# One transformer block on one core: other order of the score, value and wide steps inside a group of four

## The reference

```
x = x + cross_attention(layernorm(x), context)    # 16 heads of 16; softmax over 4096 context tokens
x = x + linear_attention(layernorm(x))            # features exp(clip(proj)), causal, 16 heads
x = x + ffn(layernorm(x))                         # silu(x Wg) * (x Wu), then Wd; hidden 768
```

## Time and profile before

| | |
|---|---|
| median of three runs | 904.28 us (903.49 to 911.03) |
| the profiled execution | 905.16 us, of which the span from first to last instruction 903.4 us |
| PE busy | 842.8 us (93%) |
| ACT busy | 533.5 us (59%) |
| DVE busy | 425.4 us (47%) |
| POOL busy | 48.4 us (5%) |
| mean granted TensorE clock | 0.985 |

### The profile page before, as it was taken

The page is one execution under the profiler, slowest core; times in us unless marked ns, Lnnn a source line. Parts: engine busy times, 40 slices in busy tenths (PEclk is TensorE's granted clock), DMA queues, the critical chain, the costliest instruction groups (busy, mean ns, idle before and its releaser), DMA issues.

```text
span 903.4 us, 20695 instructions
## 1 busy us (share of the span) xinstructions
PE 842.8 (93%) x8881; PEld 581.3 (64%) x8881; DVE 425.4 (47%) x751; ACT 533.5 (59%) x579; POOL 48.4 (5%) x76
## 2 busy tenths in 40 slices
PE   6899999999899999999899999999989999888876
PEld 6666666666566666676566666676656667657655
DVE  7433245545544446534644446434744444203663
ACT  2378787776467675656566665757556666760111
POOL 1034000000000000000000000000000000000000
PEclk9799999999999999999999999999999999999999
DMA  7487664656133334336333442446333331201000
GB/s 242 150 260 236 229 199 153 210 190 187 57 141 141 118 141 163 130 109 184 130 118 141 141 141 94 142 140 178 127 140 141 109 142 56 71 25 24 1 1 15
DMA packets 58736, 120.08 MB, mean 133 GB/s; under 512 B 21520, under 2 KB 29712, under 8 KB 55120
## 3 DMA queue, kind: packets, MB, share of 16 engines
q1 hardware_dynamic: 56848, 114.31, 37.2%
q0 software_dynamic: 1792, 4.40, 1.9%
HBM read 78.84 MB, written 37.75 MB: 129 GB/s over the span
## 4 chain that ended last, share of the span: by engine, by line
PE 77%; DVE 9%; issue 5%; DMA 4%; ACT 3%; DVEq 1%; POOL 1%; SPq 0%; POOLq 0%; ACTq 0%
PE ps_o L777 24%; PE ps_s L789 16%; PE ps_pa L576 10%; PE ps_pa L621 10%; ACT probs L1066 2%; PE ps_pa L747 2%; DMA oscr<-y 2%; PE ps_pa L722 2%; PE ps_pa L713 1%; DMA y<-oscr 1%; PE ps_pa L699 1%; PE ps_pa L651 1%; PE ps_pa L734 1%; PE ps_pa L643 1%; DVE kparts L1105 1%
## 5 line engine op out<-in xcount | busy, mean ns | idle before, releaser
L1066 ACT ACTIVATE probs<-ps_s 128x1024 f32<-128x1024 f32 x512 | 496.7, 1023 | 262.8 <-PE ps_s L789 254.4
L777 PE MATMUL ps_o<-probs,values 128*17 128x256 f32 x4096 | 257.6, 386 | 0.3 <-ACT probs L1066 0.3
L789 PEld LDWEIGHTS ps_s<-qstack,kstack 64*128 64x128 f32 x2048 | 139.1, 185 | 102.4 <-ACT probs L1066 53.2
L789 PE MATMUL ps_s<-qstack,kstack 64*128 64x256 f32 x2048 | 193.5, 307 | 7.0 <-ACT probs L1066 7.0
L777 PEld LDWEIGHTS ps_o<-probs,values 128*17 128x17 f32 x4096 | 104.4, 98 | 100.3 <-issue 12.8
L1103 DVE TENSOR_SCALAR kparts<-ps_pa,b_heads 128x512 fp32r<-128x512 f32 x64 | 48.0, 750 | 122.1 <-PE ps_pa L576 122.1
L1120 DVE TENSOR_TENSOR values<-ps_pa,bv_pair 128x512 f32<-128x512 f32 x64 | 44.1, 690 | 84.7 <-PE ps_pa L621 84.3
L621 PE MATMUL ps_pa<-wv_hi,ctx_hi 128*128 128x256 f32 x256 | 79.5, 310 | 2.6 <-DVE wv_lo L1091 2.2
L621 PE MATMUL ps_pa<-wv_lo,ctx_hi 128*128 128x256 f32 x256 | 73.2, 286 | 0.0
L621 PE MATMUL ps_pa<-wv_hi,ctx_lo 128*128 128x256 f32 x256 | 73.1, 286 | 0.0
L576 PE MATMUL ps_pa<-ctx_hi,wk_hi 128*128 128x512 f32 x128 | 56.5, 441 | 0.0
(11 more groups left out here) (252 smaller groups left out, 792.2 us busy)
## 6 DMA issues: line engine op xcount, KB each, us to landing
kstack<-kscr SPq DMA_DIRECT2D x96, 512.0 KB, 5.3
kscr<-kparts SPq DMA_DIRECT2D x64, 512.0 KB, 2.7
ctx_raw<-ctxT SPq DMA_DIRECT2D x32, 512.0 KB, 6.6
qstack<-qscr SPq DMA_DIRECT2D x12, 256.0 KB, 3.4
qscr<-qparts SPq DMA_DIRECT2D x4, 512.0 KB, 4.4
xh<-x SPq DMA_DIRECT2D x4, 256.0 KB, 5.6
kstack<-kstack SPq DMA_DIRECT2D x2, 512.0 KB, 6.0
qstack<-ksample SPq DMA_DIRECT2D x4, 256.0 KB, 3.6
```

The lines of the kernel that those rows point to most:

```text
L777: last = mm(ps_o[32 * j:32 * j + DH + 1, g * S:(g + 1) * S], values[par][:, i, head_of_step(g, j), :], prob[:, j * S:(j + 1) * S], start=b ...
L789: last = mm(ps_s[s % 2][:, j * S:(j + 1) * S], kstack[par][rows, u, i * P:(i + 1) * P], queries[rows, u, :], start=True, stop=True)
L1066: nc.scalar.activation(probs[n % AHEAD][:, :], ps_s[n % 2][:, :], ACT.Exp, scale=float(DH) ** -0.5).then_inc(fast["exp_done"], 1)
```

## The change

A quad with a wide stage gets another order on PE: two score steps, the unit and the narrow stages of all four slots, the value steps up to this quad (four of them), one score step, the wide stage, one score step. Inside such a quad the unit now stands ahead of the wide stage in all cases. So that DVE meets them in the same order, three wide stages move within their quad, to its last slot: feat0 from step 32 to 35, feat2 from 48 to 51 (behind pv0), A4 from 64 to 67. ACT's part of each feat stage comes after the last exponential of its quad. The order of TAIL, by which the last batch's stages run, changes in one place: pv0 comes ahead of feat2.

```diff
 AT = { ...
-      "feat0": 32, "feat1": 38, "A0": 42, "A1": 46, "feat2": 48, "pv0": 50, "A2": 54, "A3": 58, "pv1": 60, "feat3": 62,
-      "A4": 64, "A5": 70, ...
+      "feat0": 35, "feat1": 38, "A0": 42, "A1": 46, "pv0": 50, "feat2": 51, "A2": 54, "A3": 58, "pv1": 60, "feat3": 62,
+      "A4": 67, "A5": 70, ...
-ACT_BEHIND = {n: 1 - AT[n] % 2 if AT[n] // QUAD in WIDE_QUADS else QUAD - 1 - AT[n] % QUAD for n in FEATS + GATES}
+ACT_BEHIND = {n: QUAD - 1 - AT[n] % QUAD for n in FEATS + GATES}
...
-            def fast_slot(b, p, s):
+            def fast_slot(b, p, s, wide=True):
...
                 for name, clock in stages_at(b, p * STEPS + s):
-                    products(fast, [name], clock)
+                    if wide or name not in WIDE:
+                        products(fast, [name], clock)
...
                         if b and (p * STEPS + s) // QUAD in WIDE_QUADS:
-                            for half in (0, 2):
-                                for t in (0, 1):
-                                    fast_scores(b, q, s + half + t)
-                                for t in (0, 1):
-                                    fast_slot(b, p, s + half + t)
-                                values_up_to(n + half)
+                            for t in (0, 1):
+                                fast_scores(b, q, s + t)
+                            for t in range(QUAD):
+                                fast_slot(b, p, s + t, False)
+                            values_up_to(n)
+                            fast_scores(b, q, s + 2)
+                            for t in range(QUAD):
+                                for name, clock in stages_at(b, p * STEPS + s + t):
+                                    if name in WIDE:
+                                        products(fast, [name], clock)
+                            fast_scores(b, q, s + 3)
```

## The result

The changed kernel takes 939.73 us (median of four runs, 937.51 to 941.83), the kernel before beside it 906.18 (903.49 to 911.03). The ratio is 1.036, 95% interval 1.031 to 1.042: slower. I had forecast slower and 929, with a range of 918 to 937. The direction and the main cost were right, the size was not: 33.6 us between the medians against my 24.7, and the time is 2.7 us beyond the range. The profiled execution took 940.29 us, its span is 938.6; against the profiled execution before (905.16, span 903.4) that is 35.1.

A forecast was written before the change was run, and what follows sets the result against it. PE's own sequence was taken as the bound (93% busy). Per batch 12.6 - 1.5 - 1.8 - 1.5 = +7.8 us, three batches +23.4, tail +1.3: +24.7, giving 929 us, range 918 to 937.

The forecast's parts named there:

- Step 6: ACT and DVE in the new order: waits covered, unit behind wide stage with 0.8 us to spare; no cost counted.
- step 2: Wide stages in key-unit quads no longer wait for DVE to take keys from PSUM: gain 1.8 us per batch.
- Rival (b): Units behind wide stages wait for DVE, up to 1 us in a third of quads: 942 us; 6 in 100.
- Rival (c): Clock falls from PE idling, half of the 36 quads at the lower level: 69 us on top, 999; 3 in 100.
- Step 5: Score step n+5 behind each wide stage waits for exponential n+3: 1.05 us each, 12.6 us lost per batch.
- the 0.10 us: Part of the cost behind each wide stage: a score step after a wait costs 0.43, not 0.33, weights not loaded ahead.
- Step 1: Quads 8 to 20: 13 groups of value steps instead of 25, 0.13 us each: gain 1.5 us per batch.
- Step 3: Waits at score step 211 in quad 20 (0.64) and for exponential 192 in quad 16 (0.9) go: 1.5 us per batch.
- Step 4: PE's 1.11 us wait before feat0 for quad 7's keys stays, at quad 8's value unit: no change counted.
- Step 7: Last batch's tail: pv0 ahead of feat2 delays DVE's clip and A2's output: cost 1.3 us once.

The follow-up runs named there:

- the half exponential: Changed kernel, exponential of step n+3 in each of the 36 wide quads takes only half its tile: 920.53 us, before 905.24, ratio 1.019.
- the paired order: Changed kernel with score step n+3 ahead of the wide stage, which is now last in its quad: 929.80 us, before 905.24, ratio 1.029.
- D: Theory that in quads 8, 12, 16 DVE's first value output waits for the quad's own last value step; changed kernel without this wait: 928.84 us.
- the experiment on the value output: Changed kernel, DVE's output of a chunk's first value unit waits for eight value steps of the earlier chunk, not sixteen: 928.84 us, ratio 1.028.

## Why the prediction was wrong in size

**Where the 35 us are.** Between the two profiled executions: three stretches of 9.4 us, 28.3. Two lower-clock stretches in them, 3.0. The same once more in quads 26 and 27 of batch 3, 1.4. From the first score step of the last quad to the end of the span, 100.5 us (838.09 to 938.6) against 97.35 (806.09 to 903.4), 3.1, of which 1.4 are the order and 1.7 I put down to the clock. The rest, -0.7, is elsewhere. My sum had 23.4 for the stretches and 1.3 for the tail.

**Step 6 failed.** It said "The moved stages feat0, feat2 and A4 bring no instruction and no DMA more", which is true, and step 2 took the PE work between unit and wide stage (1.85 + 0.24 us) as enough to cover DVE's output of the unit in every quad. So the sum had nothing for a wait there. In quads 8, 12 and 16 it is not enough. `fast_values_out` waits for all value steps of the chunk before (`pv_done`), since it overwrites their buffer, and in the new order the last of these stand in the same quad, behind the unit. The old order had two or four value steps ahead of the unit. So the wide stage came 0.6 us late in quads 8 and 12 and 0.7 in quad 16, in each of three batches: 6.0 us by the experiment. With them the sum would have been 30.7 of the 33.6 us between the medians. I had looked for the waits of PE in the new order, and for one of ACT's, but not for those of DVE. Rival (b) had the right engine at the wrong place (units behind wide stages, its own 0.8 us to spare held).

**Rival (c) came, in a small form.** I gave the clock 3 in 100, all or nothing: 69 us. What happens is between: single short stretches at the lower level, some 1.5 us each, in two of three batches and in the tail. In numbers, the changed kernel ran at 0.973 to 0.978 in all nine runs, the kernel before at 0.975 to 0.988. I had leaned on one tail row with a clock of 1.00 and PE idle for 6 of 20 us; that row was true of one execution, and other executions of the kernel before go down to 0.975. With the value output's wait mended it is 0.977 to 0.985, with value steps behind the wide stage 0.981 to 0.983. Some 6 us between the two profiled executions hang on this; the sum had no term for it. That the waits of the changed kernel are the cause is not shown: with the old tail and the same waits three runs of four had 0.980 to 0.983, and the kernel with three waits mended, whose stretches leave PE idle for 1.1 us only, ran at 0.975 to 0.987. The Trainium skill ("TensorE: Matmul & The Clock Gate", A second HAM failure mode: psum-queue depth-cycling) says that short, frequent idling between groups of matmuls can make the clock swing. The two executions agree in direction: 0.50 was granted inside a stretch that had stayed at 1.00 in all three batches before. The price in this kernel is a few us.

**Step 5 was right for this order, and not the whole rule.** 1.62 us and 0.43 were measured as forecast, the half exponential gives its 0.43 us back twelve times per batch, and the waits vanish with two value steps between n+3 and n+5. But the paired order shows a second bound, which step 5 rightly set aside for its own order ("The exponential n+2 does not add"): n+2 to n+5 must hold two exponentials, 2.54 us, so that work between n+3 and n+5 alone need not end the wait. And the 0.10 us do not belong to the wait, as the last section shows; a lone score step costs them more than the second of a pair, wait or not. With D taken out, the stretch is 7.4 us longer than before, against my 7.8. That is close in part by luck: I had 0.24 us for the score step ahead of an A stage and 0.74 for the stage, and they cost 0.34 and 0.57.

**Steps 1, 3, 4 and 7 held, and step 2 but for what it took as covered.** Four value steps cost 1.85; an A stage in a key quad starts 0.34 behind its score step; quad 20's wait between 210 and 211 and quad 16's for exponential 192 are gone from the timeline; the value unit of quad 8 waits for the keys 1.0 us; the tail's order costs 1.4.

**What stays open.** Why the clock falls at one place and not at another was not tried: a filler matmul in the waits would need a free PSUM tile, and in these quads all of this kernel's are in use. Nor is it shown that idling lowered the clock here; the runs with the old tail speak against it. The 2.9 us between the medians that neither my sum nor the value output explains I put down to the clock, without a proof.

## What to carry to other kernels

With two tiles in turn between two engines, write down two distances for each new order: from a producer's step to the one that overwrites its tile, to compare with one step of the consumer plus the latencies (1.62 us here), and from the step before it, to compare with two (2.54); a quad of four steps needs other work in both of its gaps, not in one. When a step is moved, go through the waits of each engine that has a part in it, and ask of each semaphore what now stands in front of its last increment; a buffer's "all that used it are done" is the easiest to miss, and here it asked for more than is overwritten. And a kernel that sits at 97% busy still has waits worth naming: three of 0.6 to 1.1 us, mended together, gave 0.7%, a third less in the stretches than their sum, as the next wait took its share.

## What the runs showed of the hardware

A score step whose wait ends with an exponential costs 0.43 us to the next group instead of 0.33. It does so in each of the 36 quads. But it is no price of the wait: a score step that stands alone and waits for nothing costs as much in front of another kind of group, 249.79 - 249.35 = 0.44 in the experiment on the value output. 0.33 is the second of two score steps in a row (0.67 for both). The Trainium skill ("TensorE: Matmul & The Clock Gate", Step-by-step: what each phase is for) says that TensorE pulls weight loads ahead of matmuls in flight; the trace agrees, in that the weights of the A stage of quad 11 start to load at 271.92, while the score step's matmuls run from 271.69 to 272.19:

```profile
271.69 0.30 PEld L789 LDWEIGHTS ps_s<-qstack,kstack 64*128 64x128 f32 x4 [0.42 <-ACT probs L1072]
271.92 0.74 PEld L722 LDWEIGHTS ps_pa<-feat,kfeat 64*128 64x128 f32 x8
```

The first score step behind value steps, or behind a wait, has no such early start: its loads begin with its matmuls, as in the first of these lines. That this is where the 0.10 us come from is an argument, not shown.

An A stage costs 0.57 us in front of a score step (272.03 to 272.60) and 0.74 in front of value steps. I had bounded the way back to a score step between 0.2 dearer and 0.1 cheaper; it is 0.17 cheaper. The single score step ahead of the stage costs 0.34 where I had 0.24, so both together are 0.07 cheaper.

The kernel before, unchanged, ran from 901.1 to 912.3 us on one chip, with mean clocks from 0.987 down to 0.975. Differences of under 1% between two single executions say nothing in this kernel; the stretches between two score steps repeat to 0.1 us in batches at the full clock, and are the better measure.
